# A new order of the 303 parts of a period in a hybrid attention and mixture-of-experts kernel

## The reference

```python
x = x + attn_a(layernorm(x))   # log-linear attention, 32 heads of 64, state 128, silu gate, projection out
x = x + ffn(layernorm(x))      # 16-head attention (head size 8), layer norm, 8 experts with top 2, layer norm
x = x + attn_b(layernorm(x))   # 8 rolled copies and itself, each times its sigmoid gate, summed, layer norm
x = x + ffn(layernorm(x))      # the same weights as above
```

## Time and profile before

| | |
|---|---|
| median of 3 runs | 2326.39 us (2324.88 to 2329.33) |
| the profiled execution's own time | 2335.59 us |
| its span | 2333.7 us |
| mean granted TensorE clock | 0.964 of full speed |
| TensorE busy | 2126.1 us, 91% of the span |
| VectorE busy | 1719.7 us, 74% |
| ScalarE busy | 1454.2 us, 62% |
| GpSimd busy | 819.1 us, 35% |
| stores of finished items begin (L556) | 514.6 us to 2331.5 us, 16 of them |

### The profile page before, as it was taken

How to read it: one execution, slowest core, us unless ns; L and a number is a source line. 1 busy time by engine, 2 the same in 40 slices (tenths; PEclk the granted TensorE clock), 3 DMA queues, 4 the chain that set the end, 5 groups by cost and what they waited for, 6 DMA issues and landing times. The chain is left out here.

```text
span 2333.7 us, 47546 instructions
## 1 busy us (share of the span) xinstructions
PE 2126.1 (91%) x16832; PEld 1618.6 (69%) x16832; DVE 1719.7 (74%) x4431; ACT 1454.2 (62%) x3113; POOL 819.1 (35%) x1204
## 2 busy tenths in 40 slices
PE   4879889999999999999999999999999999998866
PEld 2556667777777777776777777777777777676544
DVE  6666878787887878787787878788797878755433
ACT  3555657677675766767575766767576676754332
POOL 5212332434343433424333333434333342424131
PEclk9979999999999999999999999999999999998777
DMA  5020112121202112120211212110211212010110
GB/s 152 4 47 10 38 35 47 35 48 29 43 17 45 41 36 50 35 47 8 44 37 37 48 36 48 36 37 15 45 40 36 50 35 45 15 46 21 31 34 5
DMA packets 185820, 88.01 MB, mean 38 GB/s; under 512 B 118297, under 2 KB 179873, under 8 KB 180417
## 3 DMA queue, kind: packets, MB, share of 16 engines
q1 hardware_dynamic: 185584, 84.97, 15.4%
HBM read 51.12 MB, written 33.55 MB: 36 GB/s over the span
## 5 line engine op out<-in xcount | busy, mean ns | idle before, releaser
L1186 DVE SCALAR_TENSOR_TENSOR work<-psA,c_conv_w,work 128x255 f32<-128x255 f32 (+2 forms) x810 | 329.2, 472 | 15.6 <-ACT work L926 14.7
L1261 DVE TENSOR_REDUCE nmax<-psB 128x2 f32<-128x512 f32 x512 | 315.9, 679 | 27.5 <-PE psB L741 27.3
L609 PE MATMUL psA<-xnT_a,c_w_in 128*128 128x256 f32 x1088 | 309.9, 409 | 27.7 <-ACT X L950 15.9
L1213 DVE TENSOR_TENSOR att<-att,QK 128x1024 f32<-128x1024 f32 x192 | 235.4, 1253 | 85.4 <-ACT att L963 85.2
L845 PE MATMUL psB<-c_w,hid 128*128 128x128 f32 x2048 | 280.2, 282 | 7.3 <-ACT pt L1009 5.9
L845 PEld LDWEIGHTS psB<-c_w,hid 128*128 128x128 f32 x2048 | 257.8, 194 | 41.1 <-issue 19.0
L1009 ACT ACTIVATE pt<-psB 128x512 f32<-128x512 f32 x512 | 264.4, 606 | 33.0 <-PE psB L760 33.0
L833 PE MATMUL psB<-x1T,c_w 128*128 128x256 f32 x1024 | 276.6, 398 | 6.2 <-ACT hid L1051 5.4
L963 ACT ACTIVATE att<-psA 128x512 f32<-128x512 f32 x384 | 204.5, 610 | 109.7 <-PE psA L650 83.0
L1032 ACT ACTIVATE hid<-psB,c_b 128x256 f32<-128x256 f32 x496 | 210.8, 484 | 57.8 <-PE psB L833 53.6
L609 PEld LDWEIGHTS psA<-xnT_a,c_w_in 128*128 128x128 f32 x1088 | 194.6, 201 | 72.5 <-ACT X L950 24.1
(11 more groups left out here) (246 smaller groups left out, 4275.1 us busy)
## 6 DMA issues: line engine op xcount, KB each, us to landing
qk_scr<-qparts SPq DMA_DIRECT2D x128, 192.0 KB, 2.5
q_stack<-qk_scr SPq DMA_DIRECT2D x96, 192.0 KB
k_stack<-qk_scr SPq DMA_DIRECT2D x32, 576.0 KB
lvl_scr<-work SPq DMA_DIRECT2D x32, 192.0 KB, 5.2
low<-lvl_scr SPq DMA_DIRECT2D x256, 1.5 KB
c_w_in<-in_in_wT SPq DMA_DIRECT2D x1, 2176.0 KB, 9.3
x<-in_x SPq DMA_DIRECT2D x16, 128.0 KB, 4.4
c_w<-in_W SPq DMA_DIRECT2D x2, 1024.0 KB
```

The lines of the kernel that those rows point to most:

```text
L609: e.matmul(t[:, 0:T], w_in[:, first + j * P:first + (j + 1) * P], xnT_a[:, :], start=True, stop=True).then_inc(filled[b], 1)
L1186: m = e.scalar_tensor_tensor(out=cv[:, back:], in0=t[:, 0:T - back], scalar=conv_w[:, c, tap:tap + 1], in1=cv[:, back:], op0=ALU.mult, op1 ...
L1213: e.tensor_tensor(att[:, :, :], att[:, :, :], bc(QK[:, kq, :], 1, HG), ALU.mult).then_inc(att_done, 1)
L1261: e.tensor_reduce(nmax[:, i, 2 * h2:2 * h2 + 2], t[:, :].rearrange("p (h k) -> p h k", k=T), AX.X, ALU.max).then_inc(drained[b], 1)
```

## The change

Only the string `PERIOD` changes. The same 303 parts stand in another order, and since the new text of the period begins in another place (about 67 places further on in the cycle), the lags of the parts ahead of that place are one higher; counted round the cycle most parts move by fewer than 10 places. No function is touched. In the new order `q0.1`, `lvl0.2`, `up1.6` and `down1.3` come some 15 to 70 places later against their neighbours than before, `gates0.1`, `gates0.4`, `prod0.2`, `prod0.3` and `bcp0.0` some 12 to 37 places earlier.

```diff
-load_x0.0+0 tail0.5+3 up0.0+3 ep1.0+4 fn0.0+2 relu0.0+3 ocopy1.0+4 es1.1+4 lvl0.0+1 exps1.1+4 down1.6+5 fn0.1+2
-conv0.1+1 tail0.6+3 q0.0+2 experts0.0+3 ep1.1+4 acc1.6+5 tap0.0+1 ocopy1.1+4 experts0.1+3 es1.2+4 lvl0.1+1
-exps1.2+4 down1.7+5 q0.1+2 up0.1+3 conv0.2+1 taps0.0+1 acc1.7+5 ep1.2+4 down0.0+3 tap0.1+1 es1.3+4 relu0.1+3
-down0.1+3 tap0.2+1 taps0.1+1 acc0.0+3 up0.2+3 up0.3+3 ocopy1.2+4 acc0.1+3 exps1.3+4 relu0.2+3 down0.2+3
-silu0.0+1 experts1.2+5 relu0.3+3 taps0.2+1 zgate0.0+1 acc0.2+3 up0.4+3 down0.3+3 zact0.0+1 conv0.3+1 up0.5+3
-relu0.4+3 tap0.3+1 down0.4+3 silu0.1+1 lvl0.2+1 xt0.0+1 silu0.2+1 conv0.4+1 gates0.0+0 relu0.5+3 acc0.3+3
-experts1.3+5 up0.6+3 up0.7+3 xt0.1+1 taps0.3+1 conv0.5+1 tap0.4+1 silu0.3+1 xcopy0.0+1 acc0.4+3 relu0.6+3
-down0.5+3 tap0.5+1 taps0.4+1 down0.6+3 xcopy0.1+1 relu0.7+3 zgate0.1+1 down0.7+3 xt0.2+1 taps0.5+1 zact0.1+1
-acc0.5+3 acc0.6+3 acc0.7+3 conv0.6+1 tap0.6+1 ep1.3+4 silu0.4+1 ocopy1.3+4 xcopy0.2+1 silu0.5+1 xt0.3+1
-experts0.2+3 taps0.6+1 tail1.0+4 experts0.3+3 conv0.7+1 zgate0.2+1 tap0.7+1 bcp0.0+1 taps0.7+1 xcopy0.3+1
-zact0.2+1 tail1.1+4 mix1.0+3 v0.0+2 xt0.4+1 silu0.6+1 tail1.2+4 xcopy0.4+1 zgate0.3+1 tail1.3+4 silu0.7+1
-smax0.0+2 xt0.5+1 xt0.6+1 mix1.1+3 rowmax0.0+2 zact0.3+1 xcopy0.5+1 smax0.1+2 conv0.8+1 tap0.8+1 tail1.4+4
-smax0.2+2 lvl0.3+1 lvl0.4+1 lvl0.5+1 rowmax0.1+2 lvl0.6+1 xcopy0.6+1 rowmax0.2+2 mix1.2+3 mix1.3+3 tail1.5+4
-tail1.6+4 mix1.4+3 mix1.5+3 taps0.8+1 qk0.0+1 up1.0+4 up1.1+4 relu1.0+4 relu1.1+4 mix1.6+3 experts1.0+4 mix1.7+3
-mix1.8+3 qkc0.0+1 coef0.0+1 experts1.1+4 zgate0.4+1 mix1.9+3 zact0.4+1 mix1.10+3 own0.0+1 down1.0+4 silu0.8+1
-zgate0.5+1 smax0.3+2 zgate0.6+1 zact0.5+1 acc1.0+4 rowmax0.3+2 mix1.11+3 zgate0.7+1 zact0.6+1 lvl0.7+1 up1.2+4
-relu1.2+4 zact0.7+1 maxt0.0+2 mix1.12+3 down1.1+4 acc1.1+4 up1.3+4 weigh0.0+1 weigh0.1+1 wexp0.0+1 down1.2+4
-weigh0.2+1 es0.0+2 prod0.0+1 relu1.3+4 sum0.0+1 wexp0.1+1 exps0.0+2 acc1.2+4 fn1.0+3 wexp0.2+1 down1.3+4
-own0.1+1 fn1.1+3 ep0.0+2 ocopy0.0+2 q1.0+3 gates0.1+0 prod0.1+1 xt0.7+1 es0.1+2 weigh0.3+1 own0.2+1 xcopy0.7+1
-exps0.1+2 up1.4+4 acc1.3+4 sum0.1+1 wexp0.3+1 ep0.1+2 es0.2+2 gated0.0+1 relu1.4+4 ocopy0.1+2 exps0.2+2
-gated0.1+1 prod0.2+1 gates0.2+0 down1.4+4 q1.1+3 ep0.2+2 ocopy0.2+2 es0.3+2 sum0.2+1 up1.5+4 exps0.3+2
-weigh0.4+1 acc1.4+4 up1.6+4 wexp0.4+1 own0.3+1 weigh0.5+1 prod0.3+1 gated0.2+1 sum0.3+1 wexp0.5+1 prod0.4+1
-prod0.5+1 own0.4+1 own0.5+1 sum0.4+1 ep0.3+2 weigh0.6+1 gated0.3+1 relu1.5+4 wexp0.6+1 sum0.5+1 gated0.4+1
-gates0.3+0 relu1.6+4 prod0.6+1 down1.5+4 ocopy0.3+2 gated0.5+1 acc1.5+4 tail0.0+2 weigh0.7+1 wexp0.7+1 own0.6+1
-own0.7+1 sum0.6+1 prod0.7+1 gated0.6+1 smax1.0+3 rowmax1.0+3 sum0.7+1 tail0.1+2 smax1.1+3 gated0.7+1 rowmax1.1+3
-tail0.2+2 up1.7+4 smax1.2+3 ssq0.0+1 ssq0.1+1 relu1.7+4 ssq0.2+1 ssq0.3+1 tail0.3+2 rowmax1.2+3 smax1.3+3
-gates0.4+0 outp0.0+1 tail0.4+2 rowmax1.3+3 maxt1.0+3 outp0.1+1 gates0.5+0 gates0.6+0 place0.0+0 v1.0+3 es1.0+3
-exps1.0+3 conv0.0+0 outp0.2+1
+load_x0.0+0 weigh0.5+2 acc1.4+5 exps0.3+3 gated0.1+2 sum0.3+2 gated0.2+2 wexp0.4+2 wexp0.5+2 gates0.3+1 ep0.3+3
+prod0.4+2 own0.4+2 own0.5+2 prod0.5+2 gated0.3+2 sum0.4+2 ocopy0.3+3 weigh0.6+2 relu1.5+5 wexp0.6+2 gated0.4+2
+own0.6+2 up1.6+5 relu1.6+5 prod0.6+2 tail0.0+3 sum0.5+2 gated0.5+2 weigh0.7+2 wexp0.7+2 down1.5+5 gates0.4+1
+own0.7+2 acc1.5+5 prod0.7+2 sum0.6+2 smax1.0+4 sum0.7+2 gated0.6+2 rowmax1.0+4 tail0.1+3 smax1.1+4 gated0.7+2
+rowmax1.1+4 up1.7+5 tail0.2+3 smax1.2+4 ssq0.0+2 ssq0.1+2 relu1.7+5 tail0.3+3 ssq0.2+2 ssq0.3+2 rowmax1.2+4
+smax1.3+4 outp0.0+2 tail0.4+3 rowmax1.3+4 gates0.5+1 maxt1.0+4 gates0.6+1 v1.0+4 tail0.5+3 outp0.1+2 tail0.6+3
+place0.0+1 outp0.2+2 es1.0+4 conv0.0+1 exps1.0+4 fn0.0+2 up0.0+3 experts0.0+3 ep1.0+4 relu0.0+3 experts0.1+3
+es1.1+4 conv0.1+1 ocopy1.0+4 exps1.1+4 down1.6+5 tap0.0+1 fn0.1+2 ep1.1+4 lvl0.0+1 lvl0.1+1 ocopy1.1+4 q0.0+2
+acc1.6+5 es1.2+4 conv0.2+1 down0.0+3 up0.1+3 taps0.0+1 down1.7+5 exps1.2+4 tap0.1+1 acc0.0+3 acc1.7+5 ep1.2+4
+tap0.2+1 taps0.1+1 relu0.1+3 es1.3+4 down0.1+3 ocopy1.2+4 exps1.3+4 up0.2+3 up0.3+3 acc0.1+3 relu0.2+3 silu0.0+1
+conv0.3+1 relu0.3+3 taps0.2+1 q0.1+2 down0.2+3 tap0.3+1 acc0.2+3 up0.4+3 relu0.4+3 up0.5+3 zgate0.0+1 down0.3+3
+down0.4+3 silu0.1+1 xt0.0+1 experts1.2+5 conv0.4+1 zact0.0+1 silu0.2+1 relu0.5+3 gates0.0+0 taps0.3+1 tap0.4+1
+acc0.3+3 xt0.1+1 up0.6+3 silu0.3+1 acc0.4+3 bcp0.0+1 up0.7+3 xcopy0.0+1 conv0.5+1 taps0.4+1 relu0.6+3 tap0.5+1
+down0.5+3 down0.6+3 experts1.3+5 xt0.2+1 relu0.7+3 down0.7+3 zgate0.1+1 taps0.5+1 conv0.6+1 acc0.5+3 acc0.6+3
+ep1.3+4 xcopy0.1+1 silu0.4+1 xt0.3+1 acc0.7+3 experts0.2+3 xcopy0.2+1 tap0.6+1 zact0.1+1 ocopy1.3+4 taps0.6+1
+experts0.3+3 silu0.5+1 tail1.0+4 conv0.7+1 xcopy0.3+1 tap0.7+1 tail1.1+4 taps0.7+1 mix1.0+3 xt0.4+1 tail1.2+4
+v0.0+2 zgate0.2+1 silu0.6+1 silu0.7+1 smax0.0+2 zgate0.3+1 zact0.2+1 tail1.3+4 xcopy0.4+1 xt0.5+1 mix1.1+3
+zact0.3+1 smax0.1+2 xt0.6+1 conv0.8+1 xcopy0.5+1 lvl0.2+1 rowmax0.0+2 tail1.4+4 smax0.2+2 rowmax0.1+2
+rowmax0.2+2 xcopy0.6+1 tap0.8+1 lvl0.3+1 mix1.2+3 mix1.3+3 tail1.5+4 tail1.6+4 mix1.4+3 lvl0.4+1 lvl0.5+1
+mix1.5+3 qk0.0+1 taps0.8+1 up1.0+4 up1.1+4 relu1.0+4 lvl0.6+1 relu1.1+4 mix1.6+3 experts1.0+4 mix1.7+3 mix1.8+3
+mix1.9+3 zgate0.4+1 mix1.10+3 down1.0+4 qkc0.0+1 experts1.1+4 up1.2+4 acc1.0+4 relu1.2+4 zact0.4+1 zgate0.5+1
+coef0.0+1 smax0.3+2 lvl0.7+1 zact0.5+1 own0.0+1 rowmax0.3+2 zgate0.6+1 silu0.8+1 mix1.11+3 zgate0.7+1 zact0.6+1
+zact0.7+1 down1.1+4 maxt0.0+2 weigh0.0+1 down1.2+4 acc1.1+4 wexp0.0+1 mix1.12+3 weigh0.1+1 wexp0.1+1 gates0.1+0
+up1.3+4 acc1.2+4 weigh0.2+1 es0.0+2 prod0.0+1 sum0.0+1 xt0.7+1 relu1.3+4 fn1.0+3 exps0.0+2 prod0.1+1 wexp0.2+1
+up1.4+4 fn1.1+3 own0.1+1 ep0.0+2 relu1.4+4 ocopy0.0+2 q1.0+3 weigh0.3+1 gated0.0+1 prod0.2+1 wexp0.3+1 es0.1+2
+sum0.1+1 exps0.1+2 own0.2+1 q1.1+3 down1.3+4 ep0.1+2 xcopy0.7+1 es0.2+2 acc1.3+4 ocopy0.1+2 prod0.3+1 exps0.2+2
+gates0.2+0 down1.4+4 ep0.2+2 es0.3+2 sum0.2+1 weigh0.4+1 up1.5+4 own0.3+1 ocopy0.2+2
```

## The result

The new order takes **2346.79 us** (median of 4 runs, 2346.53 to 2347.16), the old one beside it 2325.64 us (2324.03 to 2329.33). The ratio is 1.0089, 95% interval 1.0071 to 1.0106: **0.9% slower**, 21 us, where 11 us faster was forecast. The profiled execution of the new order took 2346.62 us, its span is 2344.8 us.

The account below looks back on a forecast made before the run. TensorE's work was taken to bound the kernel. A turn's -1.1 - 0.9 - 0.3 + 1.65 = -0.65 us gave -8.5 over the run, -11.5 with the clock: 2326.4 to 2315 us, own range 2306 to 2321, overall 2292 to 2347.

Parts of the forecast that it names:

- (b): At smax0.3: acc1.0 moved ahead of coef0.0, with more cover ahead of smax0.3, gains 0.9 us a turn.
- (c): At gates0.4, now between down1.5 and own0.7: gains 0.3 us a turn; other moves there, such as tail0.2 and up1.7, nothing.
- (d): At weigh0.2: 28 more table loads between wexp0.0 and wexp0.1 delay its second bank, stalling TensorE 1.65 us a turn.
- What bounds the kernel: TensorE's work sets the time, 4.9 us a turn idle; VectorE holds acc0.1 to mix1.1 at 28.5 us.
- (a): From maxt1.0 to mix1.1: reordered parts let VectorE reach acc0.1 after 22.4 us instead of 23.5, gaining 1.1 us a turn.
- (e): Behind mix1.1: a third of 8.5 us of half clock goes, 3 us gained; other end, 8 us lost at weigh0.2.
- Rival 4: At weigh0.2: two switches drain 1.38 us each, lengthening the stall to 4.4 us a turn; 2353 us, chance 0.04.
- Rival 1: At wexp0.1 and ep0.0: loads paid in full, 2.57 us a turn, VectorE's stretch unmoved; 2344 us, chance 0.24.

Follow-up runs that it names:

- kernel 1: The new order with mix1.12 no longer asking for the silu table, so 66 table loads for 94; 2314.2 us, 0.9934 of the old order.
- Kernel 7: The old order with conv0.2, down0.0, up0.1 ahead of down1.7, acc0.0 and acc1.7 ahead of taps0.1, and relu0.1 behind tap0.2; 2407.38 us.
- kernel 9: The old order with the whole stretch of 131 parts from maxt1.0 to mix1.1 taken from the new order; 2303.43 us.
- Kernel 5: The new order without the extra loads, with down1.0, experts1.1 and acc1.0 moved ahead of mix1.10; 2316.85 us.
- Kernels 6: The new order without the extra loads, with gated0.3 moved ahead of prod0.5 on VectorE; 2307.53 us.
- 10: The new order without the extra loads, with gated0.3 ahead of prod0.5 and also prod0.1 behind fn1.1 on VectorE; 2292.91 us.
- the old order's second trace: The old kernel unchanged, one more profiled execution for a second trace; 2324.65 us.
- kernel 3: The old order with only mix1.12 moved between wexp0.0 and wexp0.1, which adds the same 28 table loads; 2367.26 us.

## Why the prediction was wrong, point by point

In us a turn, the forecast was -2.30 for the order without its loads, +1.65 for the loads and -0.25 for the clock behind `mix1.1`, -0.9 in all. Measured were about +0.1 for the order (kernel 1 against the old order, the half clock set aside), +2.34 for the loads and -0.64 for the clock, +1.8 in all. So two steps failed. The larger is (b) with (c): (b) gave 0.2 us for 0.9, and (c) put at nothing what became waits at `weigh0.6`, `fn1.1`, `up1.7` and `smax1.3`; with some smaller shifts the order is 2.4 us off. The other is the price in (d), 0.7 us too low. The sign needs no more than the first: with the loads at 1.65 as forecast, the measured order would still have been slower.

**What bounds the kernel**: right. TensorE's work does, with VectorE's chain in one stretch. `acc0.1` to `mix1.1` took 28.5 us in the old order, 28.3 in the new, and 28.3 to 28.5 in every kernel, even in 7.

**(a)**: right in size and in mechanism. `acc0.1` starts 22.6 us behind `maxt1.0`, 22.4 was forecast; before it was 23.9. `maxt1.0` to `mix1.1` takes 50.89 us; 50.9 was forecast. That the two agree so well is in part luck: the step counted from 52.0 us where the trace has 52.4, and left out that `xt0.6` (0.44 us) goes behind `mix1.1`. The waits moved within the stretch, as said. But the step named five parts as its cause. Kernel 7 moved these (and `relu0.1`) and lost 80 us; kernel 9 took the whole stretch and won 27. The sum of TensorE's parts gives the end of a stretch only if each part's bank is free, and the parts that free them were moved too.

**(b)**: wrong. 0.9 us was forecast, `smax0.3` gained 0.2 (1.75 to 1.55), and `up1.2` lost as much. The step said that `acc1.0` was late behind `coef0.0`. In the new order VectorE's timeline has `mix1.8`, `mix1.9` and `mix1.10` ahead of it, a microsecond apart, each waiting 0.62 us for GpSimd, with `experts1.1` (L1326) and `acc1.0` (L1341) only behind them:

```profile
1213.08 0.43 DVE L1366 SCALAR_TENSOR_TENSOR hid<-hid,O_sb 128x256 f32<-128x256 f32 x1 [0.62 <-POOL O_sb L1477]
1214.12 0.43 DVE L1366 SCALAR_TENSOR_TENSOR hid<-hid,O_sb 128x256 f32<-128x256 f32 x1 [0.62 <-POOL O_sb L1477]
1214.46 0.42 DVE L1326 TENSOR_TENSOR ff<-psB,x 128x256 f32<-128x256 f32 x1
1214.92 0.61 DVE L1341 SCALAR_TENSOR_TENSOR ff<-psB,w_e,ff 128x128 f32<-128x128 f32 x2
```

Kernel 5 shows that `acc1.0` can be had sooner, and that it is worth nothing, since `up1.2` then waits for it.

**(c)**: `gates0.4` gained 0.58 us for 0.3. "Nothing" for the rest was wrong: `tail0.2` gained 0.25, but `up1.7` lost 0.50, `smax1.3` 0.33, `weigh0.6` 0.78, and `fn1.1` 0.64 once the loads no longer cover it. `weigh0.6` asks for the bank that `gated0.3` empties. On VectorE `gated0.3` stood behind `prod0.4` and `prod0.5` in the old order too; new is `gates0.3` (three operations, L1127 to L1133) ahead of them, so that they start with `sum0.3` and not 1.8 us before it. The old order first (`sum0.3` at 1113.78), then the new (1114.40):

```profile
1111.96 3.68 DVE L1213 TENSOR_TENSOR att<-att,QK 128x1024 f32<-128x1024 f32 x3 [1.75 <-ACT att L963]
```

```profile
1113.62 0.83 DVE L1133 SCALAR_TENSOR_TENSOR work<-work 128x640 f32<-128x640 f32 x1
1114.37 5.47 DVE L1212 TENSOR_TENSOR att<-att,QK 128x1024 f32<-128x1024 f32 x4
```

Kernels 6 and 10 show that the waits at `weigh0.6` and `fn1.1` can be had back; `up1.7` and `smax1.3` (both for VectorE's `rowmax`) no kernel tried. I had not looked past the parts that moved far. The loads and stores on SyncE were covered, as said: no wait for `k_stack` or the level weights is in the new trace.

**(d)**: right in its mechanism, too low in its price. The wait in `weigh0.2` was found in the right place for the right reason. Its size was 2.02 us (1.85 seen as idle) for 1.65: TensorE was at the bank 5.85 us behind the start of `down1.1`, not 6.4, because `mix1.12` has no instruction on TensorE either, and the 1.0 us for changes of type and waits was less; the bank was free at 7.7 us, not 8.05. And the wait was taken to end there. It was followed by 0.64 us a turn of half clock at `sum0.0`, and by 0.47 at `es0.0`, most of it in every turn and at full clock: its last two banks are those that `relu1.3` empties, which comes late behind `wexp0.1` on ScalarE. Without the loads `fn1.1` waits 0.8 us that they had covered, so they account for 2.34 us a turn (kernel 1) of their 2.57. The price of a load held: 1.283 us, and the next instruction right behind it. The drain of about 1.38 us that the Trainium skill, ScalarE: Activation LUTs, section What ACT_TABLE_LOAD costs, counts with every switch to a different set is seen in none of the kernels. Rival 4's 2353 us was near the time by accident.

**(e)**: wrong by its balance. The half clock behind `mix1.1` did go, in all of the five steady turns that had it (0.64 us a turn in the eight, 8.5 us in all, where I took 3). But it came back behind the new wait, in four of the eight turns, 0.64 us a turn at `sum0.0` alone. So the clock gave nothing; the step had named this as the other end of its range and not chosen it. And the old order's second trace has the half clock in one turn of 12, so this gain was not a steady one.

**The cases.** Rival 1, 2344 us, with its 2.57 us a turn for loads paid in full, is the nearest to what was measured, and its time is 3 us off. Its mechanism is half right: the loads were paid for (2.34), at `wexp0.1`; but VectorE's stretch did move, and `ep0.0` did not wait. The rest of its loss stood elsewhere, at `weigh0.6`, `up1.7`, `smax1.3` and at the `smax0.3` that hardly gained. So the near time is in part luck.

## What to carry to other kernels

When a list orders five engines, a rule that inserts instructions by name (here: any `mix` step asks for the silu table) is a part of the order; look for what it inserts between two parts that belong together, and count what it costs on the engine behind it and not by that engine's idle share. A move that looks worth 1 us is worth it only with the moves that free its banks: try the whole stretch, not the parts you can explain. And when a wait at one place keeps changing its name, as at `acc1.0`, stop there and take the next place, as with `gated0.3` and `fn1.1`, where two parts moved gave 21 us. Last, look at the clock before a gain is put down to the order: with the half clock set aside, the steady turns of kernel 1 and of the old order are equal to 0.1 us.

## What the runs showed of the hardware

A table load took 1.283 us in every kernel, and where the next instruction was ready it started 0.01 to 0.02 us behind it; in ScalarE's idle time 32 loads cost 1.4 us in all, within the spread of the runs. A stall of 1.85 us of TensorE was followed by half clock (0.50 granted) for some 3 us in about every second turn, but one of 1.29 us at `sum0.0` in the old order (kernel 3) was not: `sum0.0` there took its wait and 0.2 us more. The old order's steady turn differed by 0.4 us between two executions, with the half clock in five and in one of 12 turns; kernels 1 and 9 had it in none, and their turns vary little (132.3 to 133.0 and 131.1 to 131.7). So a part of what an order gives is that its clock stays up.
